# A macaron transformer layer on one core: the work ahead of the first scores in seven interleaved chains, and the side work placed anew

## What is computed

```python
x = x + 0.5 * ffn(layernorm(x))
x = x + attn(layernorm(x))
x = x + 0.5 * ffn(layernorm(x))

def ffn(x):                    # 6 experts of rank 16, the best 2 of them used, one shared
    logits = x @ router_W.T + router_b
    w = top2 of softmax(logits), divided by its sum + 1e-6
    return x @ base_W.T + base_b + (x @ shared_A.T) @ shared_B.T \
           + sum_e w[e] * (x @ routed_A[e].T) @ routed_B[e].T

def attn(x):
    k, q, v = x @ Wk.T, x @ Wq.T, x @ Wv.T            # 16 heads of 16 columns
    k, q = layernorm per head with gains and biases, times 256 ** -0.25
    att = softmax(q k^T, causal)
    return (att v) @ Wo.T + bo
```

## Time and profile before

| | us |
|---|---|
| median of 3 runs | 1170.53 |
| lowest and highest | 1167.9, 1170.67 |
| the profiled execution | 1169.52 |
| its span, first to last instruction | 1167.7 |
| PE busy, ACT busy in the span | 1065.5, 1033.0 |
| all 1056 exponentials of L1033 | 986.2 |
| first exponential starts | 95.58 |
| last exponential ends | 1134.44 |

### The profile page before, as it was taken

The page is one execution under the profiler, slowest core; times in us unless marked ns, Lnnn a source line. Parts: engine busy times, 40 slices in busy tenths (PEclk is TensorE's granted clock), DMA queues, the critical chain, the costliest instruction groups (busy, mean ns, idle before and its releaser), DMA issues.

```text
span 1167.7 us, 22502 instructions
## 1 busy us (share of the span) xinstructions
PE 1065.5 (91%) x8692; PEld 338.3 (29%) x8692; DVE 443.7 (38%) x1161; ACT 1033.0 (88%) x1162; POOL 238.8 (20%) x385
## 2 busy tenths in 40 slices
PE   2748899999999999999999999999999999999985
PEld 2533333222332232332312232232222222222223
DVE  5657664254354443523222514332310222222114
...
PEclk9779999999999999999999999999999999999997
...
GB/s 139 11 82 80 114 37 106 50 65 120 46 25 116 91 27 28 18 53 132 10 19 1 20 93 71 28 29 1 10 37 68 44 19 19 28 10 38 10 19 19
DMA packets 93174, 56.42 MB, mean 48 GB/s; under 512 B 59730, under 2 KB 90440, under 8 KB 93064
## 3 DMA queue, kind: packets, MB, share of 16 engines
...
q10 hardware_dynamic: 2132, 0.12, 0.1%
...
## 4 chain that ended last, share of the span: by engine, by line
PE 66%; ACT 16%; issue 6%; DVE 6%; DMA 3%; POOL 1%; SPq 1%; ACTq 0%; DVEq 0%; POOLq 0%
PE ps L1470 64%; ACT ring L1033 15%; DMA xnT<-area 1%; PE ps L1596 1%; PE ps L1522 1%; DVE st L1064 1%; POOL split L705 1%; DMA parts_d<-split 0%; DVE area L1118 0%; SPq L807 0%; DMA x<-in_x 0%; ACT area L997 0%; DVE area L1274 0%; DMA xnT<-att_d 0%; DMA area<-area 0%
## 5 line engine op out<-in xcount | busy, mean ns | idle before, releaser
L1033 ACT ACTIVATE ring<-ps 128x1024 f32<-128x1024 f32 x1056 | 986.2, 1085 | 39.6 <-PE ps L1470 36.2
L1470 PE MATMUL ps<-ring,vf 128*17 128x512 f32 (+3 forms) x4608 | 541.2, 561 | 4.6 <-POOL ring L956 2.2
L1470 PE MATMUL ps<-queries,keys 50*128 50x512 f16 (+3 forms) x2304 | 358.5, 365 | 29.3 <-ACT ring L1033 16.7
L1470 PEld LDWEIGHTS ps<-queries,keys 50*128 50x128 f16 x2304 | 89.6, 93 | 465.1 <-ACT ring L1033 417.9
L956 POOL TENSOR_SCALAR_AFFINE_SELECT ring<-ring 128x256 f32<-128x256 f32 (+1 forms) x224 | 104.9, 488 | 257.5 <-ACT ring L1033 254.7
L1470 PEld LDWEIGHTS ps<-ring,vf 128*17 128x17 f32 x4608 | 89.1, 96 | 198.2 <-issue 155.0
L1250 DVE SCALAR_TENSOR_TENSOR x<-ps,power,x 128x512 f32<-128x512 f32 x32 | 23.9, 750 | 178.1 <-PE ps L1470 177.9
L942 POOL TENSOR_TENSOR rstd<-var,minus_half 128x4 f32<-128x4 f32 x24 | 24.4, 1016 | 248.6 <-DVE var L1070 248.6
L1433 DVE STREAM_TRANSPOSE oT<-ps 128x512 f32<-128x512 f32 x32 | 22.9, 717 | 126.9 <-PE ps L1470 126.7
L1470 PE MATMUL ps<-baseT,xnT 128*128 128x256 f16 x384 | 55.0, 283 | 3.0 <-DVE area L1118 2.7
L1470 PE MATMUL ps<-qkT,xnT 128*128 128x512 f16 x192 | 51.0, 396 | 3.9 <-DVE xnT L1118 1.5
...
## 6 DMA issues: line engine op xcount, KB each, us to landing
...
```

Source lines behind the costliest of these rows:

```text
L1033: act.activation(probs[:, u % RING, :], bank(2 * (u % SLOTS), 2), ACTF.Exp, bias=0.0, scale=1.0).then_inc(exp_ok, 1)
L1470: return pe.matmul(o, lhsT, rhs, start=start, stop=stop, skip_group_check=True)
```

## The change

**Ahead of the first scores** there are seven chains: `w`; `f`, `g` and `h` (the fronts of blocks 0, 1 and 2, each on its own); `p` and `r` (the preparations of blocks 0 and 1); and `q`. The string is new. What remains of `r` and `h` runs beside block 0's units: 14 stages from block 1's `roots` on (13 before) and 5 of block 2's front (8 before).

**Own tiles.** So that block 1's front can run beside block 0's, it gets tiles of its own: its normed and transposed rows lie in the memory of `queries` (`early_xn`, `early_xnT`), its statistics in set 2 and its routing in set 1, which the second feed-forward uses later. The fetches of block 0 write to `queries`, so SP first waits for block 1's last `outer0`.

**Fewer small steps**: the flag takes 9 steps, and `sizes` loses one cast in each of its two calls.

**Behind the first scores** `PLACES` and `HELD` have new numbers throughout. `LONG` is 4: block 4's front runs as `ff` beside block 2's units, no longer within `prep` beside block 3's. `BACKS` moves the back parts: blocks 0, 1 and 2 run beside blocks 4, 5 and 6 (before: 3, 4 and 5), and four of them (3, 4, 5, 6) beside block 7 (before: three, with block 3's beside block 6).

```diff
-LONG = 3
+LONG = 4
-BACKS = {3: (0,), 4: (1,), 5: (2,), 6: (3,), 7: (4, 5, 6)}
+BACKS = {4: (0,), 5: (1,), 6: (2,), 7: (3, 4, 5, 6)}
-FLAG_STEPS = 11
+FLAG_STEPS = 9
+def early_chains():
+    weights = [(0, "sizes", 0)] + [(0, "weight", k) for k in range(3)] + [(0, "sizes", 1)] + [(0, "weight", k) for k in range(3, NW)]
+    return {"w": weights, "f": list(front(0, 0, 0)), "g": list(front(0, 0, 1)), "h": list(front(0, 0, 2)),
+            "p": list(prepare(0)) + list(settle(0)), "r": list(prepare(1)) + list(settle(1)), "q": [(0, "fetch", (0, g)) for g in range(NG)]}
 def side_work(c):
-    if c + 1 < NC:
-        taken = PRELUDE.count("p") - len(list(prepare(0))) - len(list(settle(0))) if c == 0 else 0
-        yield "prep", list(itertools.chain(front(0, 0, c + 1) if c >= LONG else (), prepare(c + 1), settle(c + 1)))[taken:]
-    if c + 2 <= LONG:
-        taken = PRELUDE.count("f") - 2 * len(list(front(0, 0, 0))) if c == 0 else 0
-        yield "ff", list(front(0, 0, c + 2))[taken:]
+    if c == 0:
+        yield "prep", early_chains()["r"][PRELUDE.count("r"):]
+        yield "ff", early_chains()["h"][PRELUDE.count("h"):]
+    elif c + 1 < NC:
+        yield "prep", list(itertools.chain(front(0, 0, c + 1) if c >= LONG else (), prepare(c + 1), settle(c + 1)))
+    if 1 <= c <= LONG - 2:
+        yield "ff", list(front(0, 0, c + 2))
 PRELUDE = (
-    "ffwfwfffwffwffwffffffpfpfpfpfpwpwpfpppfppfpppwpfppfppppfppppppfwpppfppqppfppppppffpqpppppppffqpp"
-    "pfpppq"
+    "ffffwffwggffgfwgfwggfwfgggwgfgfpgpwwpphghpppgppppphpprppppphprpppppppprhrpprhrhpqqhphpwprrqrrrrp"
+    "rrqrrrrr"
 )
 PLACES = {
-        (0, "prep"): (0, 0, 0, 6, 13, 19, 19, 20, 21, 40, 47, 50, 51),
-        (0, "ff"): (4, 9, 21, 34, 38, 42, 52, 59),
+        (0, "prep"): (3, 3, 3, 3, 3, 3, 8, 16, 20, 20, 30, 31, 40, 46),
+        (0, "ff"): (0, 2, 11, 22, 39),
...
+        def norm_set(K, ln, c):
+            return 2 if K is main and (ln, c) == (0, 1) else ln
+        def route_set(K, f, c):
+            return 1 if K is main and (f, c) == (0, 1) else f
+        def turned_rows(K, ln, c):
+            return early_xnT if K is main and (ln, c) == (0, 1) else xnT[ln]
+        early_xnT = queries[:, 0:4, :].rearrange("p k t -> p (k t)").rearrange("p (n s b t) -> p n s b t", n=TC, s=2, b=2)
+        early_xn = queries[:, 4:8, :].rearrange("p k t -> p (k t)").bitcast(F32).rearrange("p (n d) -> p n d", n=TC)
...
             def fetch(K, c, g):
+                if K is main and c == 0:
+                    sp.wait_ge(*main.done["outer0", (1, 1)])
...
             def sizes(K, s):
-                dve.tensor_copy(wf[:, :], wi[:, :]).then_inc(*own.up())
-                dve.wait_ge(*own.at())
-                dve.tensor_scalar(wi[:, :], wf[:, :], -0.5, 71.5, ALU.mult, ALU.add).then_inc(*own.up())
+                dve.tensor_scalar(wi[:, :], wi[:, :], -0.5, 71.5, ALU.mult, ALU.add).then_inc(*own.up())
```

195 lines of the change are left out of this document (98 added, 97 removed).

## The result

The changed kernel takes 1153.48 us (median of 4 runs, 1151.27 to 1159.17) where the kernel before, timed beside it, took 1169.97 (1167.9 to 1170.67). The ratio is 0.9859, 95% interval 0.9841 to 0.9876. Predicted were 1158.8 us, with a range of 1149 to 1169. The sign and the two places of the gain were right, and the time is 5.3 us less than said; block by block the forecast was off by up to 5.5 us in either direction, and much of that cancelled. The profiled execution took 1151.5 us, the second shortest of the four, around a span of 1149.8, which is 17.9 us less than the span before; the medians differ by 16.5.

A forecast was written before the change was run, and what follows sets the result against it. PE and ACT are nearly full, so only their waiting can be won, ahead of the first exponential and in the blocks. A lead of 11.3 us plus 0.4 from the middle part gives 11.7 less: 1158.8 us, range 1149 to 1169.

The forecast's parts named there:

- Q, the start of the projections: Opening: block 0's projections start at 49.5, 0.7 us early; bounds 1 us late to 3 us early.
- From Q to the first exponential: Projections' start to norm's end (N) 15.0 us; queries at N + 11.4; first exponential at 82.1, 13.5 us early.
- What reaches block 1: Block 1's `roots`, waiting for POOL, start at 83.9, 11.3 us early; this lead is carried on.
- I take them as covered by the 2.2 us: Block 0: late query reads and POOL's `weigh0` before the second mask cost nothing beyond the 2.2 us between 13.5 and 11.3.
- One of the prediction's own signs of being wrong: Blocks 0 and 1 together, expected still near 92 us, growing by more than 4 us would make the prediction wrong.
- Block 3: Middle part: loses 15.9 us of PE, ACT becomes the limit, takes 109.7 to 110.2 us, 10.1 less.
- Block 2: Middle part: gains 6.9 us of PE to 85.4; at share 0.966 takes 88.4 us, 7.2 more.
- Block 7: Last block: gains 9.0 us of PE to 225.9; at share 0.982 takes 230.0 us, 2.5 more.
- The rule weighed: Opening to N: four DVE steps held 0.77 us each beside POOL, N 3 us later, time 1161.9.
- The lower share of PE: Blocks 2 and 7 at PE share 0.949: 9.6 us more, 1168.4; chance 0.20, shared with a partly missing lead.
- the slower case: Blocks 2 and 7 at PE share 0.911: 23.3 us more, 1182; chance 0.13 with its surroundings above 1169.
- more than that: Block 1 follows first exponential (lead 13.5), block 7 at ACT's pace (2.5): 1154; Q 3 us early: 1151; chance 0.12.

The follow-up runs named there:

- The run with `sizes` first: Changed kernel with the first matrix `sizes` put back ahead of block 0's scaling: 1155.69 us, ratio 0.9884 to the kernel before.
- the second profile: The changed kernel, unedited, measured and profiled again on another chip: 1150.84 us, ratio 0.9825 to the kernel before.
- The run with the gap left open: Changed kernel with block 1's two `outer0` moved from beside block 0's turns to behind its first three `qk` projections: 1159.26 us, ratio 0.9905.
- The runs that take one wait away each, and both: Changed kernel with block 1's first two `heads` at 23 (was 20), 1153.74 us; block 2's `outer0` at 33 (was 22), 1155.4 us; both, 1152.91 us.

## Why the prediction was right, and where not

**What bounds the kernel.** Right. PE's and ACT's busy times didn't move; the gain is waiting time ahead of the first exponential and in block 3.

**The negated mean.** Right in both parts: 2.2 us earlier (12.62 against the 14.85 of the earlier trace rows), and given back by the end of block 0's feed-forward, whose hidden rows stand at 29.31 where they stood at 29.53. The run with `sizes` first shows that without it they would be at 31.19.

**Q, the start of the projections.** This is a term that was mis-sized: 0.7 us forecast, 4.7 measured and 5.9 in the second profile (bounds 1 late to 3 early, so outside them too). The rows of before that I hadn't priced:

```profile
41.92 3.06 PE L1522 MATMUL ps<-ident,area 128*128 128x128 f32 x12 [5.49 <-ACT area L997]
44.77 1.91 PE L1470 MATMUL ps<-xnT,ring 128*128 128x128 f32 x8
...
48.58 1.41 PE L1470 MATMUL ps<-aT,xnT 128*128 128x118 f16 x24
...
42.00:46.00 4.00, 4.00 (x18) 3.46 (x19) 1.04 (x3) 4.00 (x9) 0.23 (x1) 0.50 0.01 2
```

In the kernel before PE stood idle for 5.49 us, its clock was 0.50 behind that, and then block 1's turns, two weight matrices and block 1's `inner0` shared the way to the projections: 7.84 us from the negated mean (42.37) to Q. In the changed kernel eight transposes of 0.63 us for four and one outer product stand there, and it is 4.85 us. The negated mean itself comes 1.67 us earlier (40.70), since less of DVE's work stands ahead. So 1.7 from DVE's queue and 3.0 from PE's, 4.7 in all. I had said that block 1's front and the first weights would be over by then, and counted nothing for it. The 3.0 us are read from the order and the rows; no run puts block 1's turns back among them. The run with the gap left open shows that Q owes nothing to the filled gap, which is worth 2.2 us of clock in the projections behind it.

**From Q to the first exponential.** Right: Q to N 14.0 (forecast 15.0), third write at N + 10.8 (10.9), queries at N + 11.3 (11.4), first exponential at N + 17.2 (17.6), in both profiles of the changed kernel. In three other kernels with this order the clock made it N + 18.6.

**What reaches block 1.** The number was right in the first profile, 11.2 us against 11.3, by luck: two errors cancel. The lead was 18.8 us, not 13.5, and block 0 gave back 7.7, not 2.2. In the second profile they don't quite cancel: 20.1 us of lead, 6.1 given back, 14.0 left. The step that failed is "I take them as covered by the 2.2 us". Of the two waits it names, the late queries cost nothing that shows, since PE never waited for them; POOL's `weigh0` ahead of the second mask did hold PE's values matmuls, for 0.97 us at 81.55, and ACT waited 2.22 us before its next step. The rest it didn't name. What cost 3.9 and 4.0 us at units 9 and 10 was PE's own order, block 1's `heads` and block 2's outer product ahead of the scores, with the lower clock behind. One of the prediction's own signs of being wrong came true with it: blocks 0 and 1 together grew by 6.4 us in both profiles, from 91.8 to 98.2, where more than 4 was to mean that it is wrong. The other half of that step failed as well, that block 1's first scores keep their distance from its `roots`: `roots` came 15.6 us early (79.68), block 1's first exponential 11.2. The runs that take one wait away each, and both, show that the cost moves to the next thing: block 0 stays between 32 and 36.5 us. The 1.6 us between the two profiles of block 0 begin in the norm of block 1: three of its steps on DVE took 1.15, 0.89 and 0.89 us beside POOL's masks in the first profile, 0.69, 0.68 and 0.69 in the second, where units 4 and 5 and their masks came 1.4 us later.

**Block 3.** Right in size (11.3 for 10.1) and cause: ACT is busy 107.49 of 108.96 us, a share of 0.987. PE lost less than I said, 8.4 us and not 15.9, which doesn't matter once ACT is the limit.

**Block 2.** PE's share was right, 0.963 for 0.966, but not its work: 80.40 us instead of 85.4. Of the 60 matmuls of block 4's front that the sum counted (24 `aT`, 24 `baseT`, 12 `bT`) 9 fell into block 3's stretch, and 10 fewer scores and values matmuls lay in block 2's; the rest is that the durations overlap, as the prediction had said they might. It lost 2.2 us, not 7.2.

**Block 7.** The other way round: PE's work was right (225.63 for 225.9 us), its share wrong, 0.959 instead of 0.982. It lost 7.8 us, not 2.5. With the same PE work at other positions the share was 0.942, so it depends on the positions as well.

**Blocks 1, 4, 5 and 6** gained 5.2 us that the sum had at zero; the new numbers there do something that no run here takes apart. In sum the middle part gave 6.4 us where I had 0.4, and in this profile that is the difference between 11.7 and 17.9 us. In the second profile, with the same span, it is 3.7 us, and the front gives 14.0 instead of 11.3. So which of the two made the time smaller than forecast stays open; both profiles show a lead larger than forecast (by 5.3 and 6.6 us), larger losses in block 0 (by 5.5 and 3.9) and block 7 (by 5.3), and a smaller loss in block 2 (by 5). That these come to only 6 us in sum is luck.

**The rule weighed** (port sharing, 3 us on the way to N). N came earlier, not later, so it didn't decide. But the durations are there, in a new place. DVE's first step of block 1's `roots` takes 1.00 us beside POOL's multiplication of 0.94, where the same step at 53.52 takes 0.23:

```profile
80.13 1.00 DVE L1066 TENSOR_SCALAR tmp<-ss 128x128 int32<-128x128 int32 x1
```

The second cast of the earlier trace rows, 0.94 us before, now takes 0.17 at 27.22, as no work of POOL stands beside it. The Trainium skill, page "SBUF — State Buffer", section "Who interferes with whom", has the lock that DVE and GpSimd share; by that rule the trace agrees in both places. On the way to N no DVE step was held: all are within 0.15 us of their shortest durations up to 69 us, so the 3 us weighed there were zero. Behind it they came to some 2.5 us in the first profile (an estimate from the longer steps: 0.85 at 69.33, 0.77 at 80.13, 0.9 in the norm of block 1), of which the last stand ahead of the two long waits of block 0.

**The rivals.** The lower share of PE came true in block 7 alone (0.959 is nearer 0.949 than 0.982) and cost half of what that rival had; the slower case never came near. The measured 1153.48 us lies 1 us below the first case (1154.5 to 1163, chance 0.55), in the band of "more than that", which had 0.12. Of that rival's reasons Q early came true, by more than its 3 us; block 7 didn't stay at ACT's pace, and block 1 started later behind the first exponential, not with it. Its last figure was also 0.8 us low: Q 3 us early is 2.3 more than the 0.7 already counted, so 1151.8.
